# Graph attention over a gathered table: the features of a head in groups of two instead of four, 784 columns in a row instead of 800

## The reference, cut to what matters

```python
hs = (x @ Ws + bs).reshape(N, H, HD)            # N, H, HD = 1250, 8, 96
hd = (x @ Wd + bd).reshape(N, H, HD)
hs_e = hs[src]                                  # a row of 768 for each edge
e = leaky_relu(hs_e + hd[dst], 0.2)
logits = einsum('ehd,hd->eh', e, attn)
m = segment_max(logits, dst); ex = exp(logits - m[dst])
s = segment_sum(ex, dst)
out = segment_sum((ex / s[dst])[..., None] * hs_e, dst)
```

## Time and profile before

| | |
|---|---|
| time, median of 3 runs | 2146.78 us (2143.33 to 2149.74) |
| the profiled execution's own time | 2149.37 us |
| its span, first to last instruction | 2147.3 us |
| PE busy | 2057.0 us (96%) |
| DVE busy | 1652.7 us (77%) |
| ACT busy | 1160.0 us (54%) |
| POOL busy | 975.0 us (45%) |
| mean granted TensorE clock | 0.984 of 2.4 GHz |
| gathers (queue q0) | 298.64 MB, 44.8% of the 16 DMA engines' span |

### The profile page before, as it was taken

How to read it: one execution, slowest core, us unless ns; L and a number is a source line. 1 busy time by engine, 2 the same in 40 slices (tenths; PEclk the granted TensorE clock), 3 DMA queues, 4 the chain that set the end, 5 groups by cost and what they waited for, 6 DMA issues and landing times. The chain is left out here.

```text
span 2147.3 us, 85544 instructions
## 1 busy us (share of the span) xinstructions
PE 2057.0 (96%) x29551; PEld 1669.1 (78%) x29552; DVE 1652.7 (77%) x3737; ACT 1160.0 (54%) x3113; POOL 975.0 (45%) x1023
## 2 busy tenths in 40 slices
PE   7999999998899999999998899899999999999798
PEld 4665555555799999999997555589999999999676
DVE  5545882564699999999998764489999999999884
ACT  2101200014677777777775423477777777777584
POOL 0000010120577777777773211267777777777020
PEclk9999999999999999999999999999999999999899
DMA  6000233995788888888884224488888888888411
GB/s 202 1 0 8 82 106 122 261 277 148 226 269 270 264 276 271 270 267 277 270 271 140 90 88 135 126 252 271 271 270 269 272 262 279 272 267 271 182 58 50
DMA packets 191648, 427.41 MB, mean 199 GB/s; under 512 B 60291, under 2 KB 128841, under 8 KB 191537
## 3 DMA queue, kind: packets, MB, share of 16 engines
q0 software_dynamic: 59584, 298.64, 44.8%
q1 hardware_dynamic: 128155, 119.85, 18.3%
q10 hardware_dynamic: 3828, 7.85, 1.1%
HBM read 385.68 MB, written 29.10 MB: 193 GB/s over the span
## 5 line engine op out<-in xcount | busy, mean ns | idle before, releaser
L531 ACT ACTIVATE at_relu<-at_turned,ah_attn_size 128x512 f32<-128x512 f32 x1092 | 713.4, 687 | 308.5 <-PE at_turned L605 298.2
L507 POOL DMA_INDIRECT at_rows<-table,ah_index x360 | 425.0, 1180 | 176.2 <-POOL ah_index L495 72.0
L507 POOL DMA_INDIRECT ah_room<-table,ah_index x352 | 422.1, 1199 | 167.9 <-POOL ah_index L495 65.8
L711 DVE SCALAR_TENSOR_TENSOR at_relu<-at_relu,ah_pair_sign 128x512 f32<-128x512 f32 x546 | 377.1, 744 | 9.4 <-ACT at_relu L531 9.3
L741 DVE SCALAR_TENSOR_TENSOR sums<-sums,at_factor,at_total 128x97 f32 x1456 | 358.5, 307 | 4.5 <-PE at_total L647 1.1
L601 PE MATMUL at_turned<-ident,ah_room 128*128 128x128 f32 x2208 | 341.7, 278 | 19.0 <-PEq L1701 19.0
L601 PE MATMUL at_turned<-ident,at_rows 128*128 128x128 f32 x2160 | 331.0, 276 | 0.1
L601 PEld LDWEIGHTS at_turned<-ident,ah_room 128*128 128x128 f32 x2208 | 243.9, 142 | 39.9 <-issue 39.8
L601 PEld LDWEIGHTS at_turned<-ident,at_rows 128*128 128x128 f32 x2160 | 236.3, 141 | 19.9 <-issue 19.9
L731 DVE TENSOR_TENSOR at_spread<-at_lined,at_weight 128x1024 f32<-128x1024 bf16 x182 | 221.4, 1217 | 4.1 <-ACT at_weight L542 4.1
L605 PE MATMUL at_turned<-ah_place,dst_rows 96*128 96x128 bf16 x2208 | 216.0, 220 | 0.0
(11 more groups left out here) (315 smaller groups left out, 2904.2 us busy)
## 6 DMA issues: line engine op xcount, KB each, us to landing
at_flags<-run_flags SPq DMA_DIRECT2D x182, 64.0 KB
dst_rows<-pr_parts SPq DMA_DIRECT2D x76, 144.0 KB, 2.7
ah_place<-places SPq DMA_DIRECT2D x92, 96.0 KB
dst_rows<-local_rows SPq DMA_DIRECT2D x13, 672.0 KB, 4.9
places<-dst_rows SPq DMA_DIRECT2D x13, 672.0 KB, 6.8
at_place<-places SPq DMA_DIRECT2D x90, 96.0 KB
table<-ah_room SPq DMA_DIRECT2D x20, 400.0 KB, 4.9
ah_room<-table,ah_index POOLq DMA_INDIRECT x368
```

The lines of the kernel that those rows point to most:

```text
L507: pool.indirect_dma_start(rows[b][:, j, :], None, table, bass.IndirectOffsetOnAxis(index[b][:, j:j + 1], 0)).then_inc(gathered[b], 16)
L531: act.activation(relu[c][:], turned[chunk(b, c)][:], ACT.Relu, scale=attn_size[:, c:c + 1]).then_inc(bent, 1)
L711: dve.scalar_tensor_tensor(relu[c][:], relu[from_][:], pair_sign[:, c:c + 1], relu[c][:], ALU.mult, ALU.add).then_inc(joined, 1)
```

## The change

The group size becomes two. A head then has 48 groups of two features and a 49th with its 1 and its linear part; no column is unused. `HX` is 98, `TX` 784 columns, 3136 bytes. All views follow from the constant: chunks of 128 columns still hold the same 16 features of each head, in another order. The number of instructions stays.

```diff
 HALF = D // 2
 HK = P // H
 HW = HD + 1
-QUAD = 4
+QUAD = 2
 HX = HD + QUAD
 TX = H * HX
 HM = 4
```

## The result

The changed kernel took 2153.46 us (median of 15 runs) against 2146.14 us for the kernel before (15 runs): ratio 1.0029, 95% interval 1.002 to 1.0038. It is 6 us slower, where 4.9 us less had been forecast. The time lies within the stated range; the sign does not. The one execution that was profiled with these runs took 5330 us, some 2.5 times as long in every stage at a granted clock of 1.00 (a macro in 16.9 us), for a reason that nothing here shows, and is not used: all rows "after" are from a second profiled execution of the same file (2151.6 us, span 2149.6 us).

The account below looks back on a forecast made before the run. PE was taken to bound the loops. From the 2146.78 us median, 4.9 us saved on message columns and zero for short runs, gathers and turnovers gave 2141.9, rounded to 2142.0 us (-0.23%), range 2134 to 2157.

Parts of the forecast that it names:

- Part 1: PE's message matmuls in the loops: two columns less save 27 ns a macro, 4.9 us in all.
- Part 2: PE reading message data in runs of two: opening 49 pieces (81 ns) fits under reading 98 columns (83 ns), cost zero.
- the cheap case: Message reads on PE: opening a piece takes 1.76 ns, +9.9 us, total 2152 us; low end of a rival given 0.12.
- wrong in part 2: Profile signs in PE's messages: group spacing above 86 ns, batch up to 2.7 us, L647's mean well above 251 ns.
- The rival's dear end: Message reads on PE: cost goes by number of runs, +233 us, total 2380 us; high end of a rival given 0.12.
- The two-hit rule: SBUF reads: at least two accesses must fall in one 16-byte line for full bandwidth, making runs of two the shortest free.
- Parts 3 and 4: Gathers of 3136-byte rows gain nothing, their cost hidden; shorter runs in turnovers and small pieces on DVE and ACT cost zero.
- runs of two cost: Rival for PE's message reads: runs of two cost PE time, total 2152 to 2380 us; chance 0.12.
- what was called no change: Whole kernel's time within 0.3% (6.4 us) of before, 2140.3 to 2153.2 us; chance 0.64.

Follow-up runs that it names:

- the contiguous reads: The changed kernel with each message reading 98 contiguous columns instead of 49 runs of two (sums wrong features), against the kernel before: ratio 0.9966.
- the trial: The changed kernel plus 96-column message batches in seven memory layouts before the first layer's loop, run once quiet, once with DVE and ACT busy; runs of four 2.84 to 2.85 us.
- the other trial: The changed kernel plus quiet message batches in eight further memory layouts, some with one strip alone, run once; single numbers 164 ns a group apart, 175 together.
- the paired kind: Layout in the added batches: runs of two where pairs of heads share a 16-byte piece, against runs of four: 2.3 ns a group more quiet, 3.2 beside busy engines.
- all at one place: Runs of two with all heads at the same place: 7.9 ns a group over runs of four in added batches; as whole kernel against the one before, ratio 1.0096.

## Why the prediction was right or wrong

**Part 1 was right.** 27 ns a macro for two columns less; the contiguous reads gave 29. PE is the limit and what it saves is saved.

**Part 2 failed**, at "The opening fits under the reading, just so ... So I take zero". The opening does take as long as two columns (1.7 ns a piece, 164 ns over 96; 1.65 had been read from the earlier trace rows), so the balance was right, but a balance without slack was priced as if it had slack. The term is 11.1 us instead of zero. The prediction's own upper end of the cheap case, +9.9 us, came near it by luck: it stood for an opening of 1.76 ns, read from a count of starts at 333.08 us, and by a finer window all eight have begun by 333.07, so that the row gives 0.15 us and 1.65 ns both ways. The mechanism was another: pieces open in 1.7 ns, and the delay comes from how the strips' data lie to each other. The step that pushed that case down to a chance of 0.12 was the argument against it: "L1311's streams reach the same piece at different times, about 5 ns apart, so they opened four pieces in 1.65 ns, all that the messages need". L1311 has two groups and so a single spacing, and one spacing did not show the rate of a long row of such groups: single numbers in shared pieces took 176 ns a group in the trial, 1.8 ns a number, over 64 groups (175 in the other trial). Strips that come to the same places at different times do cost each other time. The sentence in the rival's favour, that two heads share a piece in the messages, named what mattered. Of the signs for "wrong in part 2" the spacing above 86 ns came (88.3) and a longer batch, but not a mean of L647 above 251 ns. The rival's dear end, cost by the number of runs, did not come. The two-hit rule of the Trainium skill (SBUF — State Buffer, Door 1) agrees with one strip alone, where runs of two are as fast as contiguous data (5.29 us for 5.30) and single numbers take twice the time; it says nothing of strips that share a line.

**Parts 3 and 4 were right.** The gathers moved 292.68 MB for 298.64 and no wait on one appeared. L1922 took 552 to 558 ns, L1934 953, L1828 523, all as before; L1832, once a layer, went from 840 to 870 ns, which part 4 had at nothing and which weighs 0.06 us. The six loads of `attn` went from a median of 581 to 596 ns each and stayed hidden.

**The chances** followed from part 2. The rival "runs of two cost" came in, at its cheap end, with an outcome at the border of what was called no change.

Trial and loop agree in size: in the trial the paired kind cost 2.3 ns a group quiet and 3.2 beside busy engines, which for 16 groups is 37 to 51 ns a batch, and the loop has 42 to 50; all at one place it is 7.9 x 16 = 126 ns for some 115 in the loop. What stays open is what the delay of a pair hangs on. It went from some 1 to 4 ns between stretches of the same kind, and in the loop by the place in the round of four buffers and by the length of a row (some 20 ns a macro). Since the batches repeat with the round in both layers, chance traffic in SBUF alone is not the cause; traffic in step with the loop, that of the gathers above all, was not tried by itself.

## What to carry to other kernels

Where several column strips of PE read side by side in short runs, keep their moving data out of the same 16-byte pieces (here: at four different places within each 64 bytes), or read at least four fp32 numbers from each; order the heads so that neighbours in memory are not neighbours in time. When two times balance in an estimate (81 ns under 83), count the term at risk and not at zero: there is nothing left to absorb a delay. And when a row is taken as a bound, check that it runs as long and has the same neighbours as the case, not only the same stride: one spacing of one pair of groups is not a rate.

## What the runs showed of the hardware that had not been expected

- Four strips reading the same 16-byte pieces slow each other when each takes two numbers from a piece (some 8 ns a group of 96 columns) or one (175 ns a group for 164), and not at all when each takes four (2.84 us for 32 groups, as contiguous data).
- After such a batch the next one suffers too: the head sums, contiguous and unchanged, took 8 ns longer on average over 80 macros of each loop, and some 16 in the nine macros shown.
- The size of the delay goes by where the rows lie: the same reads in rows of 800 columns for 784 took some 20 ns a macro less.
- ACT's read of 32 single numbers from SBUF (L554) went from 250 to 222 ns when their distance fell from 16 to 8 bytes; in the kernel with the heads reordered, where it takes every other one of them, 16 bytes apart again, it took 250.
